# Another order of the steps in the fourteen middle batches of a fused attention and gate network

## What is computed

```python
xn = _layernorm(x)
s = _L0_attn_ref(xn, ...)            # below
g = _silu(_L0_ffn_ref(xn, ...))      # two layers of local attention and feed forward
x = x + s * g

# _L0_attn_ref, after qkv and rope
logits = jnp.einsum('bhid,bhjd->bhij', q, k) * SCALE
logits = jnp.einsum('bhij,gh->bgij', logits, Wpre)
attn = jax.nn.softmax(logits, axis=-1)
attn = jnp.einsum('bhij,gh->bgij', attn, Wpost)
out = jnp.einsum('bhij,bhjd->bhid', attn, v)

# one layer of _L0_ffn_ref
h = shift_token(x);  q, k, v = split(h @ wqkv)
q, k = rotary_xpos(l2norm(q) * qs, l2norm(k) * ksc)
x = x + local_attention(q, k, v) @ wo
h = layernorm(shift_token(x)) @ w1 + b1;  a, g = split(h)
x = x + (a * gelu(g)) @ w2 + b2
```

## Time and profile before

| what | value |
|---|---|
| median of 3 runs | 5088.45 us |
| lowest and highest | 5087.56, 5102.07 us |
| span of the profiled execution | 5096.0 us (its own time is not given apart from its span) |
| TensorE busy | 4967.6 us, 97% |
| VectorE, ScalarE, GpSimd busy | 67%, 61%, 57% |
| DMA | 325.85 MB, 64 GB/s |
| the thirteen stretches of rows 2 | 311.4 to 316.6 us each |

### The profile page before, as it was taken

The page is one execution under the profiler, slowest core; times in us unless marked ns, Lnnn a source line. Parts: engine busy times, 40 slices in busy tenths (PEclk is TensorE's granted clock), DMA queues, the critical chain, the costliest instruction groups (busy, mean ns, idle before and its releaser), DMA issues. The chain is left out here.

```text
span 5096.0 us, 184542 instructions
## 1 busy us (share of the span) xinstructions
PE 4967.6 (97%) x76184; PEld 4084.3 (80%) x76184; DVE 3402.4 (67%) x8316; ACT 3103.6 (61%) x8073; POOL 2880.2 (57%) x2509
## 2 busy tenths in 40 slices
PE   7999999999999999999999999999999999999998
PEld 5887878878888888887887878888888888878886
DVE  7667676666766667666676766767667676676764
ACT  4656665566655666556666556665566665666655
POOL 5546565565655656555565554655546565465654
PEclk9999999999999999999999999999999999999999
DMA  2311112121111211112111211212112112111111
GB/s 86 120 72 66 70 54 75 47 69 64 55 74 46 75 58 55 74 61 68 50 67 62 74 55 53 80 47 74 55 62 70 47 74 78 44 64 70 53 60 30
DMA packets 61263, 325.85 MB, mean 64 GB/s; under 512 B 6416, under 2 KB 23824, under 8 KB 43536
## 3 DMA queue, kind: packets, MB, share of 16 engines
q1 hardware_dynamic: 49632, 297.26, 15.5%
q0 software_dynamic: 10800, 16.78, 1.7%
HBM read 288.33 MB, written 34.08 MB: 63 GB/s over the span
## 5 line engine op out<-in xcount | busy, mean ns | idle before, releaser
L1603 POOL TENSOR_TENSOR q_lo<-q_mix,q_hi 128x512 fp32r<-128x512 f32 x512 | 661.6, 1292 | 886.5 <-ACT q_hi L1059 886.4
L1072 ACT ACTIVATE probs<-bank_S,neg_max 128x512 f32<-128x512 f32 x1024 | 699.3, 684 | 727.7 <-DVE neg_max L1333 630.1
L772 PE MATMUL bank_S<-k_hi,q_lo 128*128 128x512 f32 x2048 | 880.0, 430 | 22.8 <-ACT probs L1072 13.5
L1333 DVE TENSOR_REDUCE neg_max<-bank_S 128x1 f32<-128x512 f32 x1024 | 696.0, 686 | 277.1 <-PE bank_S L774 269.7
L773 PE MATMUL bank_S<-k_lo,q_hi 128*128 128x512 f32 x2048 | 806.7, 394 | 0.5 <-issue 0.5
L774 PE MATMUL bank_S<-k_hi,q_hi 128*128 128x512 f32 x2048 | 806.3, 394 | 0.0
L789 PEld LDWEIGHTS bank_M<-mixer_n,probs 64*64 64x64 f32 x32768 | 534.0, 135 | 151.5 <-issue 132.9
L1598 POOL TENSOR_TENSOR q_mix<-q_rope,w_pre 128x256 f32<-128x256 f32 x1024 | 625.4, 638 | 43.8 <-POOL q_lo L1603 0.4
L789 PE MATMUL bank_M<-mixer_n,probs 64*64 64x64 f32 x32768 | 600.1, 221 | 8.6 <-DVE o_locT_lo L1442 3.4
L1629 POOL TENSOR_TENSOR l_probs<-l_probs,l_inv 128x1024 f32<-128x1024 f32 (+1 forms) x256 | 430.6, 1689 | 265.7 <-DVE l_inv L1436 265.1
L1614 POOL TENSOR_TENSOR inv_norms<-norms_c,minus_half 128x16 f32<-128x16 f32 x128 | 417.1, 3259 | 239.3 <-DVE norms_c L1370 237.5
(11 more groups left out here) (160 smaller groups left out, 11381.3 us busy)
## 6 DMA issues: line engine op xcount, KB each, us to landing
w_qkv_hi<-split_qkv SPq DMA_DIRECT2D x30, 1536.0 KB, 9.7
w_qkv_lo<-split_qkv SPq DMA_DIRECT2D x30, 1536.0 KB, 6.4
w_hi<-split SPq DMA_DIRECT2D x30, 1408.0 KB, 6.2
w_lo<-split SPq DMA_DIRECT2D x30, 1408.0 KB, 6.1
w_hi<-split SPq DMA_DIRECT2D x30, 768.0 KB, 5.1
w_lo<-split SPq DMA_DIRECT2D x30, 768.0 KB, 7.2
w_o_hi<-split_o SPq DMA_DIRECT2D x30, 512.0 KB, 3.7
w_o_lo<-split_o SPq DMA_DIRECT2D x30, 512.0 KB, 4.7
```

The source lines that it names most:

```text
L772: mm(bank[k][:], q_lo[q], k_hi[:, s, :], start=(s == 0), stop=False)
L1072: fn(probs[:, n % PB, :], bank[k][:], ACT.Exp, bias=neg_max[:, n % 2:n % 2 + 1], accum_out=row_sum[:, n % 4:n % 4 + 1]).then_inc(emptied[k ...
L1333: v.tensor_reduce(neg_max[:, n % 2:n % 2 + 1], bank[k][:], AX.X, ALU.max, negate=True)\
L1603: g.tensor_tensor(q_lo[:, c % QB], q_mix[:], q_hi[:, c % QB].bitcast(F32), ALU.subtract)\
```

## The change

Only the text of `ORDER` changes. Every step is there once, as before, and each keeps what it does and waits for. Batches 0 and 15 keep their orders. The core of the diff (left out: lines of both orders that the text doesn't speak of):

```diff
 ORDER = """
-expand.0 part.0 expand.1 part.1 qkv.0.0 join.0.0 scores.0 scores.1 qkv.0.1 scores.2 expand.2 bound q_turn.0.0 mixers.0
-join.0.1 part.2 k_turn.0.0 expand.3 qkv.0.2 q_turn.0.1 k_turn.0.1 scores.3 scores.4 part.3 mix.0 join.0.2 mixers.1
-expand.4 qkv.0.3 part.4 q_turn.0.2 mix.1 scores.5 join.0.3 mixers.2 k_turn.0.2 scores.6 scores.7 expand.5 mix.2
-sigmoid.0 part.5 expand.6 q_turn.0.3 mixers.3 scores.8 k_turn.0.3 part.6 scores.9 local_scores.0.0 mix.3
-local_scores.0.1 weigh.0.0 scores.10 expand.7 mixers.4 values.0 sigmoid.1 part.7 local_scores.0.2 scores.11 p_turn.0.0
-weigh.0.1 mix.4 weigh.0.2 mixers.5 scores.12 sigmoid.2 expand.8 local_values.0.0 part.8 p_turn.0.1 expand.9 scores.13
-silu mix.5 sigmoid.3 gated p_turn.0.2 local_values.0.1 mixers.6 part.9 local_scores.0.3 scores.14 scores.15
...
-out_proj.0.2 expand.13 local_values.0.6 p_turn.0.7 scores.22 local_values.0.7 mixers.10 scores.23 out_proj.0.3 mix.10
-half_turn.0 mixers.11 part.13 scores.24 expand.14 shift_turn.0 mix.11 scores.25 scores.26 mixers.12 values.2 part.14
-h_scale.0 scores.27 mix.12 mixers.13 expand.15 h_turn.0 part.15 scores.28 scores.29 mix.13 expand.16 up.0.0 mixers.14
-up.0.1 hide.0.0 hide.0.1 up.0.2 part.16 up.0.3 hide.0.2 hide.0.3 up.0.4 up.0.5 hide.0.5 hide.0.4 scores.30 expand.17
-mix.14 scores.31 scores.32 mixers.15 down.0.0 down.0.1 down.0.2 down.0.3 part.17 expand.18 part.18 mix.15 x_turn.1
-expand.19 scores.33 qkv.1.0 join.1.0 part.19 qkv.1.1 join.1.1 values.3 q_turn.1.0 k_turn.1.0 qkv.1.2 mixers.16
...
-mixers.27 part.30 scores.56 expand.31 shift_turn.1 mix.27 scores.57 scores.58 mixers.28 h_scale.1 values.6 part.31
-scores.59 mix.28 mixers.29 h_turn.1 scores.60 scores.61 mix.29 mixers.30 up.1.0 up.1.1 hide.1.0 scores.62 norm
-hide.1.1 scores.63 mix.30 mixers.31 up.1.2 up.1.3 mix.31 scale hide.1.2 hide.1.3 up.1.4 values.7 x_turn.0 up.1.5
-project.3 hide.1.5 hide.1.4 talk_k talk_q down.1.0 down.1.1 down.1.2 talk_v down.1.3
+expand.0 part.0 expand.1 part.1 expand.2 qkv.0.0 scores.0 join.0.0 part.2 expand.3 scores.1 qkv.0.1 scores.2 mixers.0
+k_turn.0.0 join.0.1 part.3 bound expand.4 q_turn.0.0 scores.3 mix.0 qkv.0.2 join.0.2 part.4 mixers.1 k_turn.0.1
+q_turn.0.1 qkv.0.3 q_turn.0.2 scores.4 k_turn.0.2 join.0.3 expand.5 scores.5 mix.1 q_turn.0.3 sigmoid.0 part.5
+scores.6 k_turn.0.3 mixers.2 local_scores.0.0 scores.7 expand.6 part.6 weigh.0.0 mix.2 local_scores.0.1 mixers.3
+scores.8 local_scores.0.2 sigmoid.1 mix.3 scores.9 expand.7 p_turn.0.0 weigh.0.1 part.7 values.0 sigmoid.2 mixers.4
+silu sigmoid.3 local_values.0.0 expand.8 scores.10 scores.11 mix.4 mixers.5 local_scores.0.3 scores.12 weigh.0.2
+scores.13 gated mix.5 mixers.6 part.8 p_turn.0.1 local_scores.0.4 scores.14 mix.6 expand.9 scores.15 local_values.0.1
...
+local_values.0.6 expand.13 p_turn.0.7 part.13 mix.10 scores.22 local_values.0.7 scores.23 expand.14 part.14 scores.24
+mixers.11 out_proj.0.3 project.0 half_turn.0 mix.11 shift_turn.0 scores.25 mixers.12 values.2 expand.15 part.15
+h_scale.0 scores.26 scores.27 mixers.13 expand.16 mix.12 h_turn.0 scores.28 scores.29 mix.13 up.0.0 hide.0.0 up.0.1
+part.16 mixers.14 hide.0.1 up.0.2 hide.0.2 up.0.3 hide.0.3 up.0.4 up.0.5 mix.14 hide.0.5 hide.0.4 scores.30 expand.17
+part.17 scores.31 mixers.15 expand.18 down.0.0 part.18 down.0.1 down.0.2 down.0.3 expand.19 mix.15 x_turn.1 scores.32
+part.19 scores.33 qkv.1.0 join.1.0 qkv.1.1 values.3 q_turn.1.0 join.1.1 k_turn.1.0 mixers.16 qkv.1.2 q_turn.1.1
+scores.34 join.1.2 k_turn.1.1 qkv.1.3 q_turn.1.2 project.1 k_turn.1.2 join.1.3 expand.20 scores.35 mix.16 q_turn.1.3
...
+local_values.1.7 part.29 scores.54 expand.30 out_proj.1.3 mix.26 half_turn.1 scores.55 shift_turn.1 mixers.27
+scores.56 scores.57 mix.27 h_scale.1 part.30 mixers.28 scores.58 values.6 norm h_turn.1 scores.59 scores.60 mixers.29
+mix.28 scale expand.31 part.31 up.1.0 mix.29 up.1.1 x_turn.0 hide.1.0 scores.61 mixers.30 scores.62 hide.1.1 up.1.2
+up.1.3 hide.1.2 hide.1.3 scores.63 mix.30 mixers.31 up.1.4 up.1.5 mix.31 talk_k hide.1.5 hide.1.4 talk_q values.7
+talk_v down.1.0 down.1.1 project.3 down.1.2 down.1.3
 """
```

28 lines of the change are left out of this document (13 added, 15 removed).

## The result

The new order takes 5154.67 us (median of four runs, 5144.49 to 5155.86), the old one beside it 5094.77 (four runs, 5087.56 to 5102.07). The ratio is 1.0114, with an interval of 1.0100 to 1.0127: some 59 us more. The forecast was 26 us more and a range up to 5140, so the direction was right and the size was not. The profiled execution has a span of 5152.8 us, 56.8 more than the earlier trace rows.

A forecast was written before the change was run, and what follows sets the result against it. TensorE, busy 97% of 5096.0 us, was taken as the bound, with VectorE 90% busy in the head. Terms summed to +2.2 us a batch, times 14 +31, less a fifth +26: 5114 us median, 5122 profiled; range 5068 to 5140.

The forecast's parts named there:

- head +2.0: Start of a batch up to local_scores.0.0: less TensorE cover, so new waiting for VectorE, +2.0 us a batch, bounds +0.8 and +2.4.
- mix.5: Behind values.0: the 0.4 us wait ahead of mix.5 goes, since sigmoids 2 and 3 run under values.0; -0.4 us a batch.
- qkv.1.0: Between the layers: x_turn.1 is followed by two scores instead of one, so qkv.1.0 waits less; -0.6 us a batch.
- down.0.0: First layer's down: a 1.6 us wait for GpSimd's hidden_lo replaces scores.32's 1.2 us wait for ScalarE; +0.4 us a batch.
- the 0.65 us forecast at mix.0 and q_turn.0.3: In the head: new TensorE waits from walking VectorE's list, 0.25 us at mix.0 and 0.4 at q_turn.0.3 a batch.
- The region up to values.0: From local_scores.0.0 to values.0: waits of 1.3 us in the old order become 1.6 in the new; +0.3 us a batch.
- The changes between full and small weights: TensorE's switches from small to full weight tiles, 63 instead of 57 a batch: +0.8 us taken, bounds 0 and 1.3.
- the smaller ones: Small shifts at half_turn.0, shift_turn.0, h_turn.0, the maxima of scores.56 and 57, and project.1: +0.5 us a batch together.
- the "issue" rows of TensorE: Sign in TensorE's list of waits: stops with no releaser total 15 to 20 us if right, instead of 30.
- Instruction packets: Fetch stops in values.0 shrink as it moves some 4 us further from loads behind qkv.0.3: -0.8 us a batch, bounds 0 and -2.
- The fifth that I took off: Off the whole sum of +31 us, because waits at neighbouring places partly replace each other; leaves +26 us.
- the 1.8 at local_scores.0.0: End of the head: local_scores.0.0 waits 1.8 us a batch for k_turn.0.3's copy, with VectorE's work setting the end.

The follow-up runs named there:

- sigmoid_late: Changed kernel with the previous batch's four sigmoids each one place later, the first out from between q_turn.0.3 and k_turn.0.3: 5158.89 us, ratio 1.0113.
- new_head: Kernel before, with the new order's steps up to and with values.0 in the middle batches, the old order behind: 5135.45 us, ratio 1.0076.
- old_head: Changed kernel with the old order up to and with sigmoid.3 (behind mix.5) in the middle batches, then the new order: 5213.82 us, ratio 1.0231.
- cover_kturn: Changed kernel with scores.7 moved ahead of local_scores.0.0 instead of behind it, in the middle batches: 5182.91 us, ratio 1.0174.
- late_loads: Changed kernel with the first layer's w_1_lo, w_2_hi and w_2_lo loads issued only when values.2 is done, in middle batches: 5131.6 us, ratio 1.0068.

## Why the prediction was wrong

**What held.** Several lines of the table came out to 0.1 us a batch: head +2.0 (measured 1.98), mix.5, qkv.1.0, and at down.0.0 a wait for GpSimd in the place of the one for ScalarE. TensorE's timeline, batch 13:

```profile
4332.53 0.39 PE L714 MATMUL bank_F<-w_hi,hidden_hi 128*128 128x256 f32 x1 [1.51 <-POOL hidden_lo L1635]
```

It was forecast at 1.6. Inside the head the sum held better than its parts: the 0.65 us forecast at mix.0 and q_turn.0.3 came at mix.1, for which nothing was forecast. The region up to values.0 was taken 0.4 too high. The changes between full and small weights with the smaller ones were 1.4 against 1.3. How much of it belongs to the changes is not settled: a scores takes 1.36 us between full steps and 1.46 with one small neighbour, and six more changes at 0.1 are 0.6 us, where 0.21 each and 0.8 in all were taken. No wait of TensorE shows for the new loads of ScalarE's tables. Most signs named in advance came: an L714 wait 14 times and more, only one L772 wait for probs, a wait of 1.5 us at the first L870 with VectorE 96% busy (24.68 of 25.77 us from 4198.29 to 4224.06). The one that would have shown the size failed: the "issue" rows of TensorE were to be 15 to 20 us and are 60, 22 of them the wait at L870 and most of the rest in `values`. A batch was to take 315 to 316 us and takes 317.4.

**The step that failed** is the term *Instruction packets*, "I take -0.8, bounds 0 and -2". It measured +1.2, outside its own bounds. Both movements were seen and written down: values.0 away from its neighbours (-0.82, as forecast) and "it brings values.2 closer to the loads behind out_proj.0.3". Only the first was priced. In the old trace values.2 already took 2.34 us in the mean for a floor of 1.92, with its loads ending some 0.4 us ahead of it (the median of the 14); that was the row to price it with. The new order ends them 0.9 to 4.3 us behind its start. I also held that a packet "may have to share the DMA engines" with loads, a slowdown; instead it doesn't start for most of their 10 us, and in batches 2, 8, 10, 12 and 14 starts only when TensorE stands still already. This term explains 28 of the 32 us that were missing, some 3 of half clock among them, of which the prediction says nothing. The fifth that I took off for waits replacing each other (of 31 us it is 6, and the forecast should have read 25) was another 5, for the measured sum shows no such replacing; the region up to values.0, taken too high, gives about as much back.

**A right number for a wrong reason** is the 1.8 at local_scores.0.0. "VectorE sets the end" led to 1.8, and a VectorE that is 96% busy looked like proof. sigmoid_late took 1.74 us of work from VectorE, and got 0.5. The row that said it was there, batch 0 with 1.1 us of wait without a sigmoid. That the number came out is luck.

**What stays open.** Why the old order has stops in values.0 and the new one none. They are in five batches (1, 2, 10, 11 and 12, where the step is 1.8 to 3.1 us longer) and no load is in flight; the loads behind qkv.0.3 ended some 4 us ahead of the step, and 8 to 9 in the new order. Counted from the start of TensorE's list, a packet border lies in the first 51 instructions of the step, or 13 ahead of it, in just these five. But the new order has it there too, in batches 9 to 11, without a stop. The steps ahead of it decide (new_head, old_head); whether by their density or by the distance to the loads was not separated. Open is also when exactly a packet gets in during a burst of loads, and why the clock falls behind some long stops and not behind others.

## What to carry to other kernels

A step of many tiny matmuls can use its instructions faster than they are brought: here 256 in 1.92 us, where a packet of 256 took about 1 us and TensorE another 1.2 to 1.6 to go on. So look at which weight loads run in the 10 us ahead of it; moving their issue behind it cost 0.1 to 0.2 us a batch here and gave back 23 of 59 us. In an order that all queues share, a step moved to cover one wait moves its work on the other engines too: cover_kturn covered 1.75 us and lost 3.3, of which 2.4 were waits and 0.9 the half clock behind them. Look at the granted clock of a stretch before you call longer matmuls a wait. And a busy engine next to a wait is not its cause until taking work from that engine shortens the wait.

## What the hardware showed

*Packets and loads.* In the DMA records of the new order a burst (w_1_lo, w_2_hi, w_2_lo) lasts 9.6 to 13.1 us, and in all 14 middle batches the first instruction packet starts 8.6 to 10.6 us after the burst began; in the old order, with w_2 issued 3.0 instead of 4.4 us behind w_1_lo, 4.0 to 8.5; in late_loads, with the three issued together, 3.2 to 7.9. So a packet can start before a burst is through, but it often has to wait: in five batches of the new order (2, 8, 10, 12, 14) it starts only after TensorE has stopped for it. The Trainium skill, "DMA: Bandwidth & Descriptors", section "Queues, rings and completion order", says that a DMA engine takes the queues in turn, but empties a whole packet of about 9 to 17 descriptors from one before it changes. A load here is 128 records on 16 engines, 8 on each. If those 8 are one such packet, the rule lets an instruction packet in behind a whole load of its engine and never inside one. No run here can show that: the records don't name the DMA engine, and in batch 5 of late_loads an instruction packet starts at 3.2 us, while rows of w_1_lo still start until 5.0.

*Time of a packet.* Its DMA takes about 1 us, and TensorE resumes 1.2 to 1.6 us after its end. `values` runs its 256 instructions in 1.92 us and `mix` its 128 in 1.09, and it is there and in a few of their small neighbours that TensorE was stopped: up to 3.4 us behind loads, up to 2.3 without. The Trainium skill, "Runtime: NRT & Kernel Launch", section "Instruction fetch mechanics", calls a border mostly hidden. That held nearly always in a scores, which has 12 instructions in 1.37 us (one such wait, of 1.1 us, in the run of the new order), and not in these.

*A round trip.* From a transpose to a matmul that reads its copy took 1.48 us with VectorE free (batch 0), 0.69 of it the copy.

*The clock.* In the middle batches the granted clock was 1.00 but for short stretches at 0.50, in the new order behind stops of 3.35, 2.7 and 2.6 us in values.2, in cover_kturn behind 1.92 and 0.69 us of waiting. A mix took 1.92 us there instead of 1.09.
